# Expert 0's first pair made the fixed first unit of the last phase, with its weights sent from the mixer's last step into memory that both phases share

## The chip, the cores and the metric

The kernel runs on 1 core of one Trainium2 chip. The metric is the device time in microseconds (us). The kernel before took 4290.4 us, the median of three runs (4289.09, 4290.40, 4294.98). A core has five engines: PE (TensorE, matrix products), DVE (VectorE), ACT (ScalarE), POOL (GpSimd) and SP (SyncE, which here only issues transfers). Each engine has its own instruction order; they wait for one another by semaphores. Transfers (DMA) run on 16 DMA engines that all issuing engines share.

## The reference

One transformer-like layer over 8 x 512 tokens of width 512, in float32:

```python
x = x + mamba(layernorm(x))     # in_proj 512->2048, conv of 4 taps, selective scan with
                                # 16 states on 1024 channels, gate, out_proj 1024->512
x = x + moe(layernorm(x))       # 8 experts, top 2 of a softmax router, weights normalised
# moe: h = silu(t @ w1[e]) * (t @ w3[e]);  y = h @ w2[e];  w1, w3: 512x1792, w2: 1792x512
```

The tokens of an expert are sorted together, so that an expert's matrices are used on many tokens at once, and the results are added back into the output with the router's weights.

## The kernel before, in words

There are two phases, each a block of the program with its own on-chip tiles.

**The mixer** (function `mixer`) goes over the tokens in 16 steps of 256 (`STEPS`). Step s scans tile s in 32 pieces (`PIECES`), prepares tile s+1, and finishes tile s-1: output projection, the sum `x1` written to `out` in DRAM (L478), second layer norm, router, and a scatter of each token's normalised row to two places in the DRAM table `rows_d` (L575, POOL). `rows_d` has one region per expert, and in it the rows come in order of arrival. From step 3 on each step also works off one tile of 128 rows of some expert (13 "early" tiles), which leaves fewer for the last phase. A 17th step, s = 16, has no scan and only finishes tile 15. In it the order is a chain: the last output product, the sum x1 on DVE (L1365), its store to `out` (L478, SP), the normalisation in place on ACT (L824, which waits for `x1_stored`, that is for the landing of that store), transposes and router logits on PE (L1024, L1171), choice and ranks on DVE and PE (L1376 to L1446), then four scatters on POOL (L575), and the plan on DVE (L1666 to L1700). The plan counts the rows left for each expert and lists pairs of tiles (2 x 128 rows) and odd tiles (128 rows). Padding rows are written behind each expert's last row by ACT (L956, L960) and SP (L528), one transfer of 257 KB per expert and one for a dummy region.

**The experts** (function `experts`) work off the plan: first all pairs (24 here), then the odd tiles (6 here). A pair is computed with a seven-product scheme (Strassen's, one level): DVE combines the weights (`combine_up`, L2120 to L2125, per quarter q of the width 1792, and `combine_down`, L2136 to L2141), POOL combines the rows (`combine_x`, L1833 to L1838), PE multiplies (`up(j)` for seven column pairs j at L2035, then `down(j)` at L2049), and DVE gathers the products (`chunk(j)`, L2147 to L2157). `up(j)` for j of 2 and more waits for `chunk(j-2)`. Between the phases all engines meet at a barrier, where each first drains. Behind it SP reads four registers from the plan, issues the first quarter of w1 and w3, waits for `scattered` and `padded`, fetches the two tiles of rows (`xr`, L1905), and issues the other quarters and w2:

```python
            n, odd = pairs_filled(sp), odds_filled(sp)
            e0 = sp.value_load(ex_i[0:1, 0:1], min_val=0, max_val=E - 1)
            r0 = sp.value_load(row_i[0:1, 0:1], min_val=0, max_val=DUMMY)
            load_up(0, e0, w13_in)
            sp.wait_ge(scattered, 16 * 2 * TT * STEPS)
            sp.wait_ge(padded, 16 * (E + 1))
            sp.dma_start(xr[:, :, :], both_rows(r0)).then_inc(x_in, 16)
```

DVE starts in this phase with `combine_up(0, q)` for the four quarters, then `chunk(0)`, `combine_down(0, 0)`, `chunk(1)` and so on. SP's order is written out by hand; it issues in that order and waits in that order.

Of the kernel before, what the change touches and what calls it, by code (L numbers as in the profile page):

```python
# [19 lines left out]
F32 = mybir.dt.float32  # L20
# [28 lines left out]
REGION = TOKENS + P  # L49
# [34 lines left out]

def planned(keep):
# [4 lines left out]
def mixer(nc, x, w_in, conv_w, w_x, w_dt, dt_bias, a_log, d_par, w_out, gate, w1, w2, w3, out, rows_d, bc_d, ident, keep,  # L90
          scattered, padded):
    with ExitStack() as ctx:
# [8 lines left out]
        win = [sb(f"win{s}", [P, DC, 2 * P]) for s in range(3)]  # L101
# [14 lines left out]
        uv = sb("uv", [P, 2 * CH * T])  # L116
# [7 lines left out]
        bc = sb("bc", [P, 2 * N, T])  # L124
        dA = [sb(f"dA{s}", [P, PN, T]) for s in range(NB)]
        hs = [sb(f"hs{s}", [P, PN, T]) for s in range(NB)]
# [233 lines left out]
        def _(sp):  # L360
# [56 lines left out]

            def step(s, odd):
# [265 lines left out]
        def _(act):  # L684
# [542 lines left out]
        def _(dve):  # L1227
# [438 lines left out]
            link(dve.tensor_tensor(ends[:, :], ebase[0:1, :], enext, ALU.subtract))  # L1666
            link(dve.tensor_scalar(ci[:, :], ends[:, :], float(P - 1), None, ALU.add))
# [35 lines left out]
def experts(nc, w1, w2, w3, out, rows_d, ident, keep, scattered, padded):  # L1703
    with ExitStack() as ctx:
# [35 lines left out]
        w13_in = [sem(f"w13_in{q}") for q in range(NQ)]  # L1740
        w2_in = [sem(f"w2_in{q}") for q in range(NQ)]
# [130 lines left out]
        def _(sp):  # L1872
# [24 lines left out]

            n, odd = pairs_filled(sp), odds_filled(sp)
            e0 = sp.value_load(ex_i[0:1, 0:1], min_val=0, max_val=E - 1)
            r0 = sp.value_load(row_i[0:1, 0:1], min_val=0, max_val=DUMMY)  # L1900
            load_up(0, e0, w13_in)

            sp.wait_ge(scattered, 16 * 2 * TT * STEPS)
            sp.wait_ge(padded, 16 * (E + 1))
            sp.dma_start(xr[:, :, :], both_rows(r0)).then_inc(x_in, 16)  # L1905
            for q in range(1, NQ):
                load_up(q, e0, w13_in)
            for q in range(NQ):
                load_down(q, e0, w2_in)
# [319 lines left out]
def build(nc, x, w_in, conv_w, w_x, w_dt, dt_bias, a_log, d_par, w_out, gate, w1, w2, w3, out):  # L2229
    rows_d = nc.dram_tensor("rows_d", (DUMMY + 2 * P, RW), F32, kind="Internal").ap()  # L2230
    bc_d = nc.dram_tensor("bc_d", (2 * N, T), F32, kind="Internal").ap()
    with ExitStack() as ctx:
        ident = ctx.enter_context(nc.sbuf_tensor("ident", [P, P], F32))
        keep = [ctx.enter_context(nc.sbuf_tensor(f"keep{i}", [P, CH * N], F32)) for i in range(2)]
        scattered, padded = [ctx.enter_context(nc.semaphore(n)) for n in ("scattered", "padded")]
        mixer(nc, x, w_in, conv_w, w_x, w_dt, dt_bias, a_log, d_par, w_out, gate, w1, w2, w3, out, rows_d, bc_d, ident, keep,
              scattered, padded)
        experts(nc, w1, w2, w3, out, rows_d, ident, keep, scattered, padded)
# [36 lines left out]
```

## Time and profile before

| | |
|---|---|
| runs, us | 4290.4 (4289.09 to 4294.98) |
| the profiled execution, us | 4298.23, its span 4296.5 |
| PE busy | 3894.7 us, 91% of the span |
| DVE, POOL, ACT busy | 3595.8, 2566.5, 2044.4 us |
| mean granted clock of TensorE | 0.958 of full speed |
| mixer | 0 to about 2442 us |
| experts | from about 2442 us to the end |
| PE's largest gap in the trace's second half | 30.7 us, before 2454.15 |

The span runs from the first to the last instruction; the execution's own time is 1.7 us longer. All rows below come from this one execution, which lies 7.8 us above the median of the runs.

### The profile page before, as it was taken

What the parts mean: (1) busy time and instruction counts of PE and PEld (TensorE: products, weight loads), DVE (VectorE), ACT (ScalarE), POOL (GpSimd) and SP (SyncE); (2) the same over time, 40 slices, a digit from 0 to 9 for tenths busy, and PEclk for the clock granted to TensorE, in tenths of its full rate; (3) what the DMA queues carried; (4) which work ended last, traced back from release to release, by engine and by line L of the source; (5) the groups of instructions that cost most, each with busy time, mean ns of one, the idle gap of its engine ahead of it and who ended that gap; (6) DMA issues with size and microseconds to landing.
All of it is one profiled execution on the core that took longest, in us unless ns stands there. A gap on an engine that the chain in (4) does not pass through costs nothing. (4 is left out here: it accounts for less than half of the span.)

```text
span 4296.5 us, 73350 instructions
## 1 busy us (share of the span) xinstructions
PE 3894.7 (91%) x25436; PEld 3379.1 (79%) x25436; DVE 3595.8 (84%) x5245; ACT 2044.4 (48%) x4314; POOL 2566.5 (60%) x2169
## 2 busy tenths in 40 slices
PE   6687889889888988998997599999999999999998
PEld 5565677677767777776776399999999999999886
DVE  5999999999999999999999588878888788788600
ACT  7677777777777777777776111111111111111100
POOL 3677778767877787787776244545545445455300
PEclk9888899999999999999998799999999999999999
DMA  4112353544445454535443455555655655555595
GB/s 162 64 40 94 114 178 114 172 163 134 153 162 170 126 162 159 176 117 173 163 138 113 160 195 183 187 176 181 195 179 183 188 174 187 179 183 191 169 313 194
DMA packets 422582, 694.12 MB, mean 162 GB/s; under 512 B 19680, under 2 KB 209760, under 8 KB 414048
## 3 DMA queue, kind: packets, MB, share of 16 engines
q1 hardware_dynamic: 406160, 655.24, 45.7%
q0 software_dynamic: 14768, 34.41, 4.2%
q8 instruction: 110, 1.80, 0.2%
q10 hardware_dynamic: 1440, 1.81, 0.1%
q14 instruction: 104, 0.85, 0.1%
HBM read 927.54 MB, written 45.95 MB: 227 GB/s over the span
## 5 line engine op out<-in xcount | busy, mean ns | idle before, releaser
L635 POOL TENSOR_TENSOR hs<-hs,bc 128x1024 f32<-128x1024 f32 x512 | 1215.4, 2374 | 312.5 <-DVE hs L1347 290.5
L1347 DVE TENSOR_TENSOR_SCAN hs<-dA,pU 128x1024 f32<-128x1024 f32 x512 | 1168.9, 2283 | 46.2 <-ACT dA L754 24.0
L754 ACT ACTIVATE dA<-delta,aneg 128x255 f32<-128x255 f32 x2048 | 852.2, 517 | 36.4 <-DVE hs L1347 33.5
L1146 PE MATMUL pY<-ident,hs 128*128 128x128 f32 x4096 | 564.2, 285 | 237.6 <-POOL hs L635 237.3
L1146 PEld LDWEIGHTS pY<-ident,hs 128*128 128x128 f32 x4096 | 486.9, 147 | 344.5 <-POOL hs L635 170.5
L1330 DVE TENSOR_TENSOR pU<-pZ,bc 128x1024 f32<-128x1024 f32 x512 | 629.8, 1230 | 30.5 <-issue 0.5
L1822 POOL TENSOR_TENSOR hsum<-hT 128x128 f32<-128x128 f32 x168 | 153.1, 911 | 585.5 <-DVE hT L2174 585.5
L1030 PE MATMUL pM<-xnT,win 128*128 128x256 f32 x1680 | 414.2, 403 | 32.1 <-DMA win<-in_w_in 26.3
L1030 PEld LDWEIGHTS pM<-xnT,win 128*128 128x128 f32 x1680 | 334.8, 205 | 83.2 <-issue 29.5
L2035 PE MATMUL ps<-xT,w1s 128*128 128x128 f32 x2688 | 357.1, 276 | 7.9 <-POOL xt L1838 4.2
L2035 PE MATMUL ps<-xt,su 128*128 128x128 f32 x2688 | 356.8, 276 | 0.0
L2035 PE MATMUL ps<-xt,w3s 128*128 128x128 f32 x2688 | 355.0, 275 | 0.0
L1013 PE MATMUL pE<-xf,ew 128*128 128x128 f32 x2912 | 342.7, 276 | 0.0
L2035 PEld LDWEIGHTS ps<-xT,w1s 128*128 128x128 f32 x2688 | 330.8, 193 | 9.8 <-POOL xt L1838 4.6
L1013 PEld LDWEIGHTS pE<-xf,ew 128*128 128x128 f32 x2912 | 333.8, 193 | 1.7
L2035 PEld LDWEIGHTS ps<-xt,su 128*128 128x128 f32 x2688 | 328.9, 193 | 0.0
L2035 PEld LDWEIGHTS ps<-xt,w3s 128*128 128x128 f32 x2688 | 327.2, 192 | 0.0
L1981 ACT ACTIVATE m<-ps 128x256 f32<-128x256 f32 x168 | 64.0, 381 | 535.3 <-PE ps L2035 535.3
L2049 PE MATMUL ps<-w2s,hT 128*128 128x256 f32 x1008 | 299.9, 379 | 0.0
L1975 ACT ACTIVATE cc<-cc 128x512 f32<-128x512 f32 x168 | 105.9, 630 | 368.5 <-DVE cc L2153 368.5
L2147 DVE TENSOR_TENSOR ut<-ps,m 128x256 f32<-128x256 f32 x168 | 70.6, 420 | 232.9 <-PE ps L2035 231.4
L658 POOL TENSOR_TENSOR xc<-xc,uv 128x512 f32<-128x512 f32 x180 | 216.5, 1203 | 10.9 <-POOL uv L652 5.8
(347 smaller groups left out, 7374.0 us busy)
## 6 DMA issues: line engine op xcount, KB each, us to landing
w1s<-in_w SPq DMA_DIRECT2D x165, 1024.0 KB
w3s<-in_w SPq DMA_DIRECT2D x165, 1024.0 KB
w2s<-in_w SPq DMA_DIRECT2D x165, 1024.0 KB
ew<-in_w SPq DMA_DIRECT2D x273, 512.0 KB, 4.1
win<-in_w_in SPq DMA_DIRECT2D x128, 512.0 KB, 4.7
bc<-bc_d SPq DMA_DIRECT2D x64, 1024.0 KB, 10.3
w1s<-in_w SPq DMA_DIRECT2D x55, 512.0 KB
w3s<-in_w SPq DMA_DIRECT2D x55, 512.0 KB
```

The source lines that it names most:

```text
L635: pool.tensor_tensor(hs[b][:, :, :], hs[b][:, :, :], bc[:, N + g * PN:N + (g + 1) * PN, :], ALU.mult)\
L658: pool.tensor_tensor(xcf[:, 2 * pair:2 * pair + 2, :], xcf[:, 2 * pair:2 * pair + 2, :], y[:, 2 * k:2 * k + 2, k:k + T], ALU.add).then_inc ...
L754: e = act.activation(dA[k % NB][:, i, 1:T], delta[:, c, 1:T], ACT.Exp, scale=aneg[:, c, n:n + 1])
L1013: m = pe.matmul(pEup[:, w, k, :], part[:, d, k * P:(k + 1) * P], exT[:, d, :], start=d == 0, stop=d == DC - 1)
L1030: m = pe.matmul(ps[:, h, :], w[:, d, h * P:(h + 1) * P], rowsT[:, d, :], start=d == 0, stop=d == DC - 1)
L1146: m = pe.matmul(pY[c % 2][:, t * P:(t + 1) * P], hs[k % NB][:, i, t * P:(t + 1) * P], ident[:, :], start=g == 0 and i == 0 and t == 0, sto ...
L1330: dve.tensor_tensor(pU[:, :, :], pDx[:, :].rearrange("p (a t) -> p a t", a=1).to_broadcast([P, PN, T]), bc[:, g * PN:(g + 1) * PN, :], ALU ...
L1347: dve.tensor_tensor_scan(hs[b][:, :, :].rearrange("p n t -> p (n t)"), dA[b][:, :, :].rearrange("p n t -> p (n t)"), pU[:, :, :].rearrange ...
L1822: pool.tensor_tensor(hs[:, j, 0, :], hT[:, j, 2, :], hT[:, j, 3, :], ALU.add).then_inc(hs_step, 1)
L1975: act.activation(cc[j % 2][:, 0:2, :], cc[j % 2][:, 0:2, :], ACT.Silu).then_inc(silu, 1)
L2035: m = pe.matmul(part(s, product)[:, h * P:(h + 1) * P], a(d, cols), b(d), start=d == 0, stop=d == KH - 1)
L2049: m = pe.matmul(part(DOWNS, product), a, b, start=j == 0 and product[1] == 0, stop=j == JN - 1 and (product[1] == 1 or product == M1))
```

## The change

On-chip memory: the mixer's `bc`, `dA`, `hs`, `uv` and `win` and the experts' `w1s`, `w3s`, `w2s` and `xr` become views of one tile `shared`, which lives through both phases. (In a list of instructions of the changed kernel they therefore all read as `shared`.) In the 17th step SP waits until POOL has weighed and PE has summed the last scan piece, and issues all eight transfers of expert 0's w1 and w3 (`first_up`), ahead of the store of x1; after its four padding transfers it issues the four of w2 (`first_down`). In the plan, expert 0's rows left are raised to at least 129, which gives it at least one pair; so the first pair is always expert 0's. For that its region gets 128 more rows of room, and ACT writes one more tile of padding. Behind the barrier SP reads only the row number, waits, and fetches `xr`; it reads the rest of the registers afterwards.

```diff
-REGION = TOKENS + P
+REGION = TOKENS + 2 * P
+WORDS = (W_BC, W_DA, W_HS, W_UV, W_WIN) = (2 * N * T, NB * PN * T, NB * PN * T, 2 * CH * T, 3 * DC * 2 * P)
+def expert_weights(shared):
+    w1s = shared[:, 0:DC * M].rearrange("p (d m) -> p d m", m=M)
+    w3s = shared[:, DC * M:2 * DC * M].rearrange("p (d m) -> p d m", m=M)
+    w2s = shared[:, 2 * DC * M:2 * DC * M + MK * D].rearrange("p (k d) -> p k d", d=D)
...
+            def first_up():
+                sp.wait_ge(weighed, PIECES * STEPS)
+                sp.wait_ge(summed, PIECES * STEPS)
+                sp.wait_ge(e_h, ROUNDS * EARLY)
+                for q in range(NQ):
+                    lo, n = WCH[q]
+                    for ws, w in ((w1s, w1), (w3s, w3)):
+                        sp.dma_start(ws[:, :, lo:lo + n], w[0:D, lo:lo + n].rearrange("(c p) m -> p c m", p=P))\
+                          .then_inc(w13_in[q], 16)
+            def first_down():
+                for q in range(NQ):
+                    lo, n = WCH[q][0] // P, WCH[q][1] // P
+                    sp.dma_start(w2s[:, lo:lo + n, :], w2[lo * P:(lo + n) * P, :].rearrange("(k p) d -> p k d", p=P))\
+                      .then_inc(w2_in[q], 16)
...
+                if s == STEPS:
+                    first_up()
                 if back:
                     hold(x1_ready, TT * r + TT)
                     sp.dma_start(tokens(out, r), rows_of(r)[:, :, 0:D]).then_inc(x1_stored, 16)
...
                 sp.dma_start(rows_d[bass.ds(r, P), :], pad).then_inc(padded, 16)
+            first_down()
             sp.wait_ge(x1_stored, 16 * STEPS)
...
                 act.dma_start(rows_d[bass.ds(r, P), :], pad).then_inc(padded, 16)
+                if e == 0:
+                    act.dma_start(rows_d[bass.ds(r + P, P), :], pad).then_inc(padded, 16)
...
             link(dve.tensor_tensor(ends[:, :], ebase[0:1, :], enext, ALU.subtract))
+            link(dve.tensor_scalar(ends[:, 0:1], ends[:, 0:1], float(P + 1), None, ALU.max))
...
+            r0 = sp.value_load(row_i[0:1, 0:1], min_val=0, max_val=DUMMY)
+            sp.wait_ge(scattered, 16 * 2 * TT * STEPS)
+            sp.wait_ge(padded, 16 * (E + 2))
+            sp.dma_start(xr[:, :, :], both_rows(r0)).then_inc(x_in, 16)
             n, odd = pairs_filled(sp), odds_filled(sp)
-            e0 = sp.value_load(ex_i[0:1, 0:1], min_val=0, max_val=E - 1)
-            r0 = sp.value_load(row_i[0:1, 0:1], min_val=0, max_val=DUMMY)
-            load_up(0, e0, w13_in)
-            sp.wait_ge(scattered, 16 * 2 * TT * STEPS)
-            sp.wait_ge(padded, 16 * (E + 1))
-            sp.dma_start(xr[:, :, :], both_rows(r0)).then_inc(x_in, 16)
-            for q in range(1, NQ):
-                load_up(q, e0, w13_in)
-            for q in range(NQ):
-                load_down(q, e0, w2_in)
```

SP's order in the mixer's last step, before the change (`xc` holds the last tile's x1, the transfer from `in_x` is its residual input):

```order
L434 DMA ew<-in_w 128x2x512
L509 DMA xc<-in_x 128x2x512 [waits x1_ready,y_turned]
L478 DMA out<-xc 128x2x512 [waits x1_ready]
L527 TENSOR_LOAD pad_i [waits pad_idx,pad_set]
```

The same place on SP after the change (`shared<-in_w` are the eight transfers of w1 and w3):

```order
L467 DMA ew<-in_w 128x2x512
L544 DMA xc<-in_x 128x2x512 [waits x1_ready,y_turned]
L441 DMA shared<-in_w 128x4x512 [waits e_h,summed,weighed]
L441 DMA shared<-in_w 128x4x512 x5
L441 DMA shared<-in_w 128x4x256 x2
L513 DMA out<-xc 128x2x512 [waits x1_ready]
L562 TENSOR_LOAD pad_i [waits pad_idx,pad_set]
```

Eight transfers now stand between SP and the store of x1.

SP's order from its last padding transfer over the barrier, before (`rows_d<-xf` is padding, `keep` holds the plan):

```order
L528 DMA rows_d<-xf 128x514
L92 UNCONDITIONAL_BRANCH [waits weights_in,consts_in,x1_stored]
L1871 UNCONDITIONAL_BRANCH [waits barrier_Pool_Activation_PE_DVE_SP_release]
L1793 TENSOR_LOAD keep
...
L1797 TENSOR_LOAD keep
...
L1899 TENSOR_LOAD keep
...
L1900 TENSOR_LOAD keep
...
L1878 DMA w1s<-in_w 128x4x512
L1878 DMA w3s<-in_w 128x4x512
L1905 ISA [waits padded,scattered]
L1905 DMA xr<-rows_d 128x2x514
```

The same place after the change (`shared<-in_w` is w2, `shared<-rows_d` the two tiles of rows):

```order
L563 DMA rows_d<-xf 128x514
L448 DMA shared<-in_w 128x4x512 x3
L448 DMA shared<-in_w 128x2x512
L103 UNCONDITIONAL_BRANCH [waits weights_in,consts_in,x1_stored]
L1905 UNCONDITIONAL_BRANCH [waits barrier_Pool_Activation_PE_DVE_SP_release]
L1932 TENSOR_LOAD keep
L1932 ISA x2
L1935 ISA [waits padded,scattered]
L1935 DMA shared<-rows_d 128x2x514
```

Four transfers of w2 stand ahead of the barrier, and the fetch of the rows comes after one register read and no weights. PE's and POOL's orders are as before; ACT has one more padding transfer, DVE one more instruction in the plan.

## Rows read from the trace of the kernel before

**Rows 1.** Timeline of PE (start us, us, engine, line, tiles, [idle before <- releaser]):

```profile
2394.06 1.91 PE L1146 MATMUL pY<-ident,hs 128*128 128x128 f32 x16
...
2454.15 1.97 PE L2019 MATMUL ps<-ident,xr 128*128 128x128 f32 x8 [30.70 <-DMA xr<-rows_d]
2460.32 2.08 PE L2035 MATMUL ps<-xT,w1s 128*128 128x128 f32 x8 [4.20 <-POOL xt L1838]
...
2473.82 1.06 PE L2035 MATMUL ps<-xt,w3s 128*128 128x128 f32 x8
2475.92 1.13 PE L2035 MATMUL ps<-xT,w1s 128*128 128x128 f32 x8 [1.04 <-DVE cc L2157]
...
2503.85 1.13 PE L2035 MATMUL ps<-xT,w1s 128*128 128x128 f32 x8 [2.69 <-DVE cc L2157]
```

**Rows 2.** The chain that ended last, from 2500 us on (start us, us, what):

```profile
2503.85 8.12 PE ps L2035 x56
...
2534.00 43.77 PE ps L2035 x392
...
2599.80 43.77 PE ps L2035 x392
```

**Rows 3.** The sequencers' instructions of L92, the barrier (engine, count: ns, start):

```profile
L92 POOLq DRAIN  x1: 14330/14330/14330, 2427.8 to 2427.8; - x1
...
L92 DVEq DRAIN  x1: 17/17/17, 2432.1 to 2432.1; - x1
```

**Rows 4.** Timeline of SP's issues:

```profile
2406.82 0.39 SPq L478 DMA_DIRECT2D out<-xc  x1
2425.57 4.59 SPq L528 DMA_DIRECT2D rows_d<-xf  x4
2444.71 0.41 SPq L1878 DMA_DIRECT2D w1s<-in_w  x1
...
2446.21 0.37 SPq L1905 DMA_DIRECT2D xr<-rows_d  x1
...
2448.95 4.48 SPq L1878 DMA_DIRECT2D w3s<-in_w  x1
...
2456.20 2.53 SPq L1878 DMA_DIRECT2D w3s<-in_w  x1
```

**Rows 5.** Timeline of DVE:

```profile
2409.37 0.15 DVE L1266 SCALAR_TENSOR_TENSOR nb<-pZ,mv 128x2 f32<-128x2 f32 x1
...
2431.68 0.17 DVE L1700 CAST keep<-delta 1x39 int32<-1x39 f32 x1
2452.76 1.23 DVE L2120 TENSOR_TENSOR su<-w3s 128x1024 f32<-128x1024 f32 x1 [20.92 <-DMA w3s<-in_w]
...
2466.04 1.23 DVE L2120 TENSOR_TENSOR su<-w3s 128x1024 f32<-128x1024 f32 x1 [1.16 <-DMA w3s<-in_w]
...
2473.24 0.41 DVE L2147 TENSOR_TENSOR ut<-ps,m 128x256 f32<-128x256 f32 x1
...
2478.22 0.42 DVE L2147 TENSOR_TENSOR ut<-ps,m 128x256 f32<-128x256 f32 x1
```

**Rows 6.** Timeline of ACT at the second layer norm of the last tile:

```profile
2409.69 1.52 ACT L824 ACTIVATE xc<-xc,nb,rs 128x512 f32<-128x512 f32 x2 [1.24 <-DMA out<-xc]
```

**Rows 7.** Windows: PE, PEld, DVE, ACT, POOL busy us, PEclk, DMA share, GB/s:

```profile
2397.50:2405.00 7.50, 6.98 (x20) 3.26 (x19) 1.04 (x2) 0.77 (x1) 4.58 (x12) 1.00 0.45 105
...
2425.00:2437.50 12.50, 0.00 (x0) 0.00 (x0) 5.95 (x32) 0.00 (x0) 4.05 (x4) 0.50 0.85 254
2437.50:2442.50 5.00, 0.00 (x0) 0.00 (x0) 0.00 (x0) 0.00 (x0) 0.00 (x0) 0.50 0.00 0
2447.50:2460.00 12.50, 1.97 (x8) 1.57 (x8) 5.17 (x5) 1.08 (x2) 2.59 (x4) 0.50 1.05 392
...
2503.85:2508.80 4.95, 4.95 (x30) 4.95 (x31) 4.85 (x11) 1.01 (x2) 2.99 (x5) 0.66 0.98 372
```

**Rows 8.** Instructions on `xr`, the odd tiles' transposes (ns, first and last start):

```profile
L2074 PE MATMUL ps<-ident,xr x28: 272/273/323, 4047.6 to 4272.2; 128*128 128x128 f32 x28
```

More of the change, by code:

```diff
@@ L82, in ge @@
         eng.wait_ge(sem, value)
+WORDS = (W_BC, W_DA, W_HS, W_UV, W_WIN) = (2 * N * T, NB * PN * T, NB * PN * T, 2 * CH * T, 3 * DC * 2 * P)
[3 more added lines that the diff above has]
+    w2s = shared[:, 2 * DC * M:2 * DC * M + MK * D].rearrange("p (k d) -> p k d", d=D)
+    xr = shared[:, 2 * DC * M + MK * D:2 * DC * M + MK * D + 2 * RW].rearrange("p (r w) -> p r w", w=RW)
+    return w1s, w3s, w2s, xr
 def planned(keep):
@@ L90, in mixer @@
 def mixer(nc, x, w_in, conv_w, w_x, w_dt, dt_bias, a_log, d_par, w_out, gate, w1, w2, w3, out, rows_d, bc_d, ident, keep,
-          scattered, padded):
+          scattered, padded, shared, w13_in, w2_in):
     with ExitStack() as ctx:
@@ L100, in mixer @@
         wgate = sb("wgate", [P, DC, E])
-        win = [sb(f"win{s}", [P, DC, 2 * P]) for s in range(3)]
+        starts = [sum(WORDS[:i]) for i in range(len(WORDS) + 1)]
+        own = [shared[:, starts[i]:starts[i + 1]] for i in range(len(WORDS))]
+        bc = own[0].rearrange("p (n t) -> p n t", t=T)
+        dA = [own[1][:, b * PN * T:(b + 1) * PN * T].rearrange("p (n t) -> p n t", t=T) for b in range(NB)]
+        hs = [own[2][:, b * PN * T:(b + 1) * PN * T].rearrange("p (n t) -> p n t", t=T) for b in range(NB)]
+        uv = own[3]
+        win = [own[4][:, i * DC * 2 * P:(i + 1) * DC * 2 * P].rearrange("p (d q) -> p d q", q=2 * P) for i in range(3)]
         convw = sb("convw", [P, CH, K])
@@ L115, in mixer @@
         state = keep[0][:, :].rearrange("p (c n) -> p c n", n=N)
-        uv = sb("uv", [P, 2 * CH * T])
         vsp, usp = uv[:, 0:CH * T], uv[:, CH * T:2 * CH * T]
@@ L123, in mixer @@
         ysum = [sb(f"ysum{i}", [P, T]) for i in range(2)]
-        bc = sb("bc", [P, 2 * N, T])
-        dA = [sb(f"dA{s}", [P, PN, T]) for s in range(NB)]
-        hs = [sb(f"hs{s}", [P, PN, T]) for s in range(NB)]
         head = keep[1][:, :].rearrange("p (c n) -> p c n", n=N)
@@ L416, in lead_in @@
                     sp.dma_start(dst[tuple([slice(None)] * len(dst.shape))], src).then_inc(weights_in, 16)
+            w1s, w3s, w2s, _ = expert_weights(shared)
+            def first_up():
[12 more added lines that the diff above has]
+                      .then_inc(w2_in[q], 16)
             def step(s, odd):
@@ L1700, in _, with experts @@
             link(dve.tensor_copy(ex_i[:, :], ex[:, :]))
-def experts(nc, w1, w2, w3, out, rows_d, ident, keep, scattered, padded):
+def experts(nc, w1, w2, w3, out, rows_d, ident, keep, scattered, padded, shared, w13_in, w2_in):
     with ExitStack() as ctx:
@@ L1739, in experts @@
         x_in = sem("x_in2")
-        w13_in = [sem(f"w13_in{q}") for q in range(NQ)]
-        w2_in = [sem(f"w2_in{q}") for q in range(NQ)]
         su_step = sem("su_step")
@@ L2234, in build @@
         keep = [ctx.enter_context(nc.sbuf_tensor(f"keep{i}", [P, CH * N], F32)) for i in range(2)]
+        shared = ctx.enter_context(nc.sbuf_tensor("shared", [P, sum(WORDS)], F32))
         scattered, padded = [ctx.enter_context(nc.semaphore(n)) for n in ("scattered", "padded")]
+        w13_in = [ctx.enter_context(nc.semaphore(f"w13_in{q}")) for q in range(NQ)]
+        w2_in = [ctx.enter_context(nc.semaphore(f"w2_in{q}")) for q in range(NQ)]
         mixer(nc, x, w_in, conv_w, w_x, w_dt, dt_bias, a_log, d_par, w_out, gate, w1, w2, w3, out, rows_d, bc_d, ident, keep,
-              scattered, padded)
-        experts(nc, w1, w2, w3, out, rows_d, ident, keep, scattered, padded)
+              scattered, padded, shared, w13_in, w2_in)
+        experts(nc, w1, w2, w3, out, rows_d, ident, keep, scattered, padded, shared, w13_in, w2_in)
 def kernel(**inputs):
```

5 lines of the change are left out of this document (1 added, 4 removed).

## The prediction

> **What bounds the kernel now.** I read the page first: PE is busy 91% of the span, and the 40 slices show one dip, near 2400 us, where the two phases meet. The timeline of PE then gives the place: after its small products of the router PE has nothing until 2454.15, 30.70 us that end with the landing of `xr`, and another 4.20 us until POOL has combined the rows; only at 2460.32 does the first pair begin [rows 1]. The chain that ended last says what a gain there is worth: from 2503.85 on it is PE's products one after the other, 43.77 us for the seven `up(j)` of each pair, 65.80 us from pair to pair [rows 2]. So what moves `up(6)` of the first pair (2503.85) moves the end by as much, and nothing later gives it back or adds to it. The change is to be followed along one path: scan's end, layer norm, router, barrier, `xr`, first pair, `up(6)`.
>
> Three places on it matter. (1) The layer norm of the last tile on ACT starts at 2409.69 [rows 6]; its scale and shift came from DVE at 2409.37 + 0.15 = 2409.52 [rows 5], so the landing of the store issued at 2406.82 [rows 4] was only 0.2 us later than the other input: it costs nothing now, but any delay of it is paid in full. (2) The barrier: DVE drains at 2432.1, but POOL's drain, behind the four scatters, ends at 2427.8 + 14.33 = 2442.1 [rows 3], though the DMA engines carry nothing from 2437.5 to 2442.5 [rows 7]. POOL sets the barrier. (3) The first pair: DVE combines weights as they land (20.92 us idle, then 1.16) and starts `chunk(0)` at 2473.24, later than PE needs it: PE waits 1.04 us for it at 2475.92, and 2.69 us at 2503.85 for a DVE that is still late [rows 1, 5].
>
> **The change part by part: what it delays.** `first_up` can start when PE has summed the last piece, 2394.06 + 1.91 = 2395.97 [rows 1]; say 2396.1. It issues six transfers of 1.049 MB and two of 0.524, 7.34 MB. Are the 0.52 MB of the store held up by them? The nearest rows: the same stream was issued from 2444.71 on; `xr` was issued at 2446.21 behind 2.10 MB of it and landed at 2454.15, 1.39 us after the quarter ahead of it (2452.76), and with 5.24 MB more issued behind it [rows 1, 4, 5]. That is one queue, worked off in order. So the store lands behind all 7.34 MB. Rate: 392 GB/s in 2447.5 to 2460 [rows 7]. Overhead: the first 2.10 MB took 2452.76 - 2444.71 = 8.05 us, of which 2.10/0.392 = 5.35 is data and 2.7 is start and finish. Alone the store would land at 2396.1 + 2.7 + (7.34 + 0.52)/0.392 = 2418.9. But scatters and the last early tile's addition run there too: 0.45 of the engines' time in 7.5 us, 3.4 us, at 105 GB/s, 0.79 MB, which at 392 is 2.0 us [rows 7]. The first gives 2422.3, the second 2420.9. Issuing does not set it: the last of the eight took its turn at 2456.20 + 2.53 = 2458.73, 14.0 us after the first [rows 4], which here is 2410.1, well before the data is through. I take 2420.9: the layer norm and all behind it 2420.9 - 2409.7 = **11.2 us later**, with ends of 9.2 and 12.6. POOL's scatters, the drain and the barrier all hang on that chain and shift with it.
>
> `first_down`: 3.67 MB of w2 behind SP's padding, while POOL's scatters are being written. SP's issue is no cost, since SP is through with padding at 2430.16 and the barrier at 2442.1 waits for POOL. What it may do is slow the scatters, and with them the drain. The DMA engines are 0.85 busy over 12.5 us there already [rows 7]; the scatters share with padding from two queues now, and would share with w2 only for what padding leaves. I take 1 us; ends 0 and 9.4 (all of w2 ahead of the last scatter, 3.67/0.392). ACT's extra padding transfer and DVE's extra instruction (about 0.2 us, as its neighbours) lie under POOL's drain, which ends 10 us after DVE's; if that cover went, they would cost a microsecond.
>
> **What it brings.** All in the times of before, as if the barrier stayed at 2442.1. SP's four register reads and start took until 2444.71, 0.6 us each, so with one read `xr` goes out at about 2443.0 instead of 2446.21. Is the queue free then? The padding and scatters keep the engines busy 0.85 x 12.5 = 10.6 us from about 2426.3 on, one more padding tile adds 0.9 (0.26 MB at 254/0.85, some 300 GB/s), w2 adds 9.4: w2 has landed at 2426.3 + 20.9 + 1.1 = 2448.3 and `xr` 1.4 behind it at 2449.7, instead of 2454.15: **4.5 us earlier**. With an empty queue it would be 2443.0 + 2.7 + 1.35 = 2447.1, 7.0 earlier; the low end is 3.5.
>
> The way from `xr` to `up(0)` (6.17 us: transposes, ACT, POOL) stays, so `up(0)` starts at 2455.8. `up(0)` and `up(1)` took 2473.82 + 1.06 - 2460.32 = 14.56 us, of which `up(1)` 6.25 (43.77/7) and `up(0)`, begun at the lower clock, 8.3. DVE: after its two register reads it begins at 2443.5 with weights that are all there; q2 and q3 took 2473.24 - 2466.04 = 7.2 us, 4.8 and 2.4 by size, so the four quarters take 16.8 and end at 2460.3, 13 us earlier than before. `chunk(0)` then no longer waits for DVE's weights but for `up(0)` (2464.1), and `chunk(1)` for `up(1)` (2470.4), before at 2478.22: **7.8 us earlier**. PE takes `up(2)` at 2470.4 without its 1.04 us, and is ready for `up(6)` at 2495.6; DVE, full from `chunk(1)` on and as long as before (25.6 us), lets it go at 2503.85 - 7.8 = 2496.0. That leaves a wait of 0.4 instead of 2.69. Behind the 2.69 the granted clock was 0.66 over 5 us [rows 7], and 56 products took 8.12 us [rows 2] instead of 6.25; behind the wait of 1.04 nothing of the kind is seen. So I count 1.9 us for a dip that does not come. Gain: 7.8 + 1.9 = **9.7 us**, ends 6.8 (3.5 by `xr`, the rest as above, no clock) and 12.2 (10.3 by a free queue, and the clock).
>
> **Sum.** 11.2 + 1.0 - 9.7 = +2.5 us. The profiled execution would take 4298.2 + 2.5 = 4300.7; it lies 7.8 above the median of the runs, so by the median 4292.9. The change in short: 13 us of weights are taken off DVE's way and 4.5 off PE's, and the same bytes are put in front of the one transfer for which the router waits.
>
> **The rivals.** *The store is not held up* (faster). Its packets would have to pass the weights. Then only the gain is left, 1.0 - 9.7 = -8.7: 4281.7. For it: completion counts per transfer, and the store writes where the loads read. Against: `xr` in the same queue landed in its place, not early. Chance 0.12.
>
> *The scatters are held up by w2* (slower). Place: POOL's drain. Price: up to 9.4 us, so 11.2 + 9.4 - 9.7 = +10.9: 4301.3. It decides as soon as the last scatter lands later than the drain would end anyway; the drain ended 5 us after the engines fell idle, so either there is that much room, or the drain counts from the last landing and has none. For it: the 14.33 us, whose cause no row names. Against: padding stood beside the scatters before as well. The Trainium skill, *DMA: Bandwidth & Descriptors*, section on queues, rings and completion order, speaks for it: each DMA engine takes turns between the queues packet by packet, and a transfer's completion mark "lands only after every earlier write from that SDMA engine, across its queues". By that rule the scatters' marks come behind whatever part of w2 was served before them, and the sum would move from +2.5 towards +10.9. No row here has weights beside scatters, so the trace neither bears it out nor refutes it. Chance 0.13.
>
> *`xr` finds its queue free*: w2 is through by the barrier, for instance because the barrier is later for another reason. The gain is then 12.2, the sum without the 1 us -1.0: 4289.4. Chance 0.10.
>
> *The forced pair is one more unit of work*: if expert 0 had at most 128 rows left, an odd tile (224.6/6 = 37.4 us from 4047.6 to 4272.2 [rows 8]) becomes a pair of 65.8: +28.4 + 2.5, 4321.3. Against: 24 pairs and 6 odd tiles over eight experts are near 6.8 tiles each. Chance 0.02.
>
> **How the numbers follow.** The forecast, 4292.9 with 4288 to 4298 as its own range, has 0.63. About 0.2% (8.6 us) is what a measurement of this kernel can tell from no change, so the bounds are 4281.8 and 4299.0. Faster: most of the first rival and a little of the third, 0.10. Slower: most of the second, the fourth, and the forecast's upper edge with a store that is held longer, 0.14. The rest, 0.76, is no change. The range: from the first rival's upper half to the full price of the second, 4283 to 4302.
>
> **What would show it.** In the profile after: the store's landing (the wait of ACT's layer norm, L860) about 11 us later than the scan's end asks for; right if 23 to 26 us lie between the last L1146-like product and the layer norm (13.7 before), wrong if under 16. POOL's drain ends 32 to 34 us after the layer norm starts (32.4 before); more than 36 is the second rival. From the barrier to the landing of `xr` 7 to 8 us (12 before), with the DMA engines busy up to it; from there 6.2 to `up(0)`. DVE's `combine_up` runs without a wait, 17 us. At `up(6)` a wait under 1 us and a granted clock near 1.0. From there to the end the same length as before, 1792.7 us. The prediction is wrong as a whole if the store lands in 3 us behind the stream, or if any gap in the steady pairs appears.

## The result and the profile after

The changed kernel took 4304.34 us (median of 10 runs, 4301.55 to 4314.38), the kernel before 4294.66 (10 runs, 4289.09 to 4297.10): ratio 1.0026, 95% interval 1.0018 to 1.0034. It is slower, by 9.7 us of the medians, and clear of the noise; 4292.9 had been forecast, with a range to 4302. The ratio and its interval are worked out from all runs, so the ratio is not the quotient of the two medians. A second timing of the same kernel beside its variants gave 1.0035 (1.0021 to 1.0048). One execution of experiment 9 took 17760.9 us and one of experiment 10 took 9054.8 us; neither is in a ratio, and without them the medians of the two are 4291.0 and 4293.9.

Its profiled execution has a span of 4312.6 us, 16.1 more than that of before. Not all of it is the change. The scan's last product ends at 2401.67 instead of 2395.97, in a part whose instructions are the same; over the 13 executions profiled for this study that point came anywhere between 2387.8 and 2401.7. So both traces are compared from the scan's end on, that is from the end of the last product that sums the scan's pieces.

SP's issues in the profile after (start us, us, engine, line, tiles):

```profile
2401.73 15.56 SPq L441 DMA_DIRECT2D shared<-in_w  x8
2417.33 2.58 SPq L513 DMA_DIRECT2D out<-xc  x1
2443.81 4.95 SPq L563 DMA_DIRECT2D rows_d<-xf  x4
2448.80 9.15 SPq L448 DMA_DIRECT2D shared<-in_w  x4
2463.89 0.40 SPq L1935 DMA_DIRECT2D shared<-rows_d  x1
```

These answer to [rows 4]. The store of x1 is issued only when the eight transfers have been: 15.66 us after the scan's end, where it was 10.85 before, so 4.8 us of its delay arise while SP still issues. From its issue to its landing it then takes 10.61 us instead of 2.87, which is the other 7.7. What the DMA engines carried meanwhile, from 2401.7 to 2428 (queue: packets, MB, share of the 16 engines' time; q1 has SP's transfers, q0 POOL's scatters and addition):

```profile
q1 hardware_dynamic: 4496, 7.86, 85.7%
q0 software_dynamic: 304, 0.79, 10.3%
```

Of the 26.3 us the engines spent 22.5 on the weights and the store and 2.7 on POOL's transfers. ACT and DVE beside the stream, with the idle time and its releaser in brackets, answer to [rows 5, 6]:

```profile
2427.94 1.52 ACT L860 ACTIVATE xc<-xc,nb,rs 128x512 f32<-128x512 f32 x2 [13.80 <-DMA out<-xc]
```

```profile
2415.06 0.15 DVE L1304 SCALAR_TENSOR_TENSOR nb<-pZ,mv 128x2 f32<-128x2 f32 x1
...
2464.70 1.22 DVE L2147 TENSOR_TENSOR su<-shared 128x1024 f32<-128x1024 f32 x1 [14.39 <-issue]
...
2474.03 1.75 DVE L2147 TENSOR_TENSOR su<-shared 128x1024 f32<-128x1024 f32 x1
2475.81 1.63 DVE L2149 TENSOR_TENSOR su<-su,shared 128x1024 f32<-128x1024 f32 x1
...
2488.55 0.42 DVE L2174 TENSOR_TENSOR ut<-ps,m 128x256 f32<-128x256 f32 x1 [5.26 <-PE ps L2062]
```

Scale and shift are there at 2415.21, and ACT waits until 2427.94 for the landing alone. Later DVE finds all weights in place and combines without a wait for them; at 2474 its instructions of 1.22 us begin to take 1.6 to 1.75. The drain of POOL at the barrier, answering to [rows 3]:

```profile
L103 POOLq DRAIN  x1: 16857/16857/16857, 2446.0 to 2446.0; - x1
```

And PE, answering to [rows 1]:

```profile
2399.76 1.91 PE L1184 MATMUL pY<-ident,shared 128*128 128x128 f32 x16
...
2470.31 1.97 PE L2046 MATMUL ps<-ident,shared 128*128 128x128 f32 x8 [28.61 <-DMA shared<-rows_d]
2479.74 2.07 PE L2062 MATMUL ps<-xT,shared 128*128 128x128 f32 x8 [7.46 <-POOL xt L1872]
...
2520.50 1.13 PE L2062 MATMUL ps<-xT,shared 128*128 128x128 f32 x8 [0.78 <-DVE cc L2184]
```

The rows land 7.45 us after the drain's end instead of 12.0, as forecast, but from there to the first product it is 9.43 us instead of 6.17: PE waits 7.46 us for POOL's `xt`, before 4.20. The reason stands in POOL's timeline. First the four subtractions of `combine_x` before, then after:

```profile
2457.33 0.77 POOL L1833 TENSOR_TENSOR xt<-xT 128x256 f32<-128x256 f32 x1 [26.28 <-ACT xT L1969]
2458.06 0.72 POOL L1834 TENSOR_TENSOR xt<-xT 128x256 f32<-128x256 f32 x1
2458.74 0.72 POOL L1836 TENSOR_TENSOR xt<-xT,xt 128x256 f32<-128x256 f32 x1
2459.54 0.72 POOL L1838 TENSOR_TENSOR xt<-xT,xt 128x256 f32<-128x256 f32 x1
```

```profile
2473.49 1.21 POOL L1867 TENSOR_TENSOR xt<-xT 128x256 f32<-128x256 f32 x1 [24.31 <-ACT xT L1996]
2474.66 1.70 POOL L1868 TENSOR_TENSOR xt<-xT 128x256 f32<-128x256 f32 x1
2476.32 1.70 POOL L1870 TENSOR_TENSOR xt<-xT,xt 128x256 f32<-128x256 f32 x1
2478.10 1.59 POOL L1872 TENSOR_TENSOR xt<-xT,xt 128x256 f32<-128x256 f32 x1
```

The same work takes 6.20 us instead of 2.93, and that is the whole growth of 3.26 us: from the rows' landing to ACT's copies it is 2.01 us in both traces. In the kernel before, DVE was idle just then, waiting for the second quarter of the weights (from 2457.5 to 2459.55). In the changed kernel it has them and works. A small piece of this stood already in the trace of before: the one DVE instruction that ran beside POOL's last subtraction (2459.54) took 1.79 us, the next one 1.23.

```profile
2459.55 1.79 DVE L2120 TENSOR_TENSOR su<-w3s 128x1024 f32<-128x1024 f32 x1 [2.03 <-DMA w3s<-in_w]
2461.38 1.23 DVE L2122 TENSOR_TENSOR su<-su,w1s 128x1024 f32<-128x1024 f32 x1
```

At `up(6)` PE's wait is 0.78 us instead of 2.69. In the window rows (PE, PEld, DVE, ACT, POOL busy, PEclk, DMA share, GB/s) the granted clock behind it is full, where [rows 7] had 0.66:

```profile
2520.50:2525.50 5.00, 5.00 (x45) 5.00 (x46) 4.90 (x11) 1.01 (x2) 3.06 (x5) 1.00 0.88 301
```

The later pairs are as before, 65.80 us each, in the chain that ended last (answering to [rows 2]):

```profile
2549.02 43.77 PE ps L2062 x392
2614.82 43.77 PE ps L2062 x392
```

The stages, each the difference of two such rows, in us; the last column but one is their sum, from the scan's end to the end of the span. "Forecast" gives the prediction's own stages.

| | scan's end to layer norm | to drain's end | to rows landed | to up(0) | to up(6) | to pair 2 | to the end | sum |
|---|---|---|---|---|---|---|---|---|
| before | 13.72 | 32.44 | 12.02 | 6.17 | 43.53 | 29.99 | 1762.66 | 1900.5 |
| forecast | 24.9 | 33.4 | 7.5 | 6.2 | 40.2 | 28.1 | 1762.7 | 1903.0 |
| after | 26.27 | 34.92 | 7.45 | 9.43 | 40.76 | 28.35 | 1763.75 | 1910.9 |
| difference to before | +12.55 | +2.48 | -4.57 | +3.26 | -2.77 | -1.64 | +1.09 | +10.4 |

The last +1.09 is mostly the first odd tile, whose products in the chain take 28.02 us after and 27.14 before; why is not shown.

### The profile page after: what moved, and what is told of

It is laid out like the page before. It is cut to its first block and busy times, and to the rows that moved or that the text cites. A ratio compares the mean times of both kernels' runs of the same rounds, so it can differ in the third digit from the quotient of the medians.

```text
span 4312.6 us, 73332 instructions
## 1 busy us (share of the span) xinstructions
PE 3900.8 (90%) x25436; PEld 3380.3 (78%) x25436; DVE 3596.9 (83%) x5246; ACT 2044.5 (47%) x4314; POOL 2574.7 (60%) x2169
## 5 line engine op out<-in xcount | busy, mean ns | idle before, releaser
L671 POOL TENSOR_TENSOR shared<-shared 128x1024 f32<-128x1024 f32 x512 | 1215.0, 2373 | 306.5 <-DVE shared L1385 284.5
L1385 DVE TENSOR_TENSOR_SCAN shared<-shared,pU 128x1024 f32<-128x1024 f32 x512 | 1168.5, 2282 | 49.1 <-ACT shared L790 26.8
L790 ACT ACTIVATE shared<-delta,aneg 128x255 f32<-128x255 f32 x2048 | 852.4, 517 | 37.2 <-DVE shared L1385 34.8
L1184 PE MATMUL pY<-ident,shared 128*128 128x128 f32 x4096 | 564.2, 285 | 233.2 <-POOL shared L671 232.9
L1184 PEld LDWEIGHTS pY<-ident,shared 128*128 128x128 f32 x4096 | 486.0, 146 | 341.9 <-POOL shared L671 169.1
L1368 DVE TENSOR_TENSOR pU<-pZ,shared 128x1024 f32<-128x1024 f32 x512 | 629.8, 1230 | 30.5 <-issue 0.5
L1068 PE MATMUL pM<-xnT,shared 128*128 128x256 f32 x1680 | 416.9, 405 | 34.7 <-DMA shared<-in_w_in 28.9
L1068 PEld LDWEIGHTS pM<-xnT,shared 128*128 128x128 f32 x1680 | 336.7, 206 | 86.8 <-issue 32.1
L2062 PE MATMUL ps<-xT,shared 128*128 128x128 f32 x2688 | 356.6, 276 | 8.2 <-POOL xt L1872 7.5
L2062 PE MATMUL ps<-xt,shared 128*128 128x128 f32 x2688 | 355.0, 275 | 0.0
```

The lines of the kernel that those rows point to most:

```text
L671: pool.tensor_tensor(hs[b][:, :, :], hs[b][:, :, :], bc[:, N + g * PN:N + (g + 1) * PN, :], ALU.mult)\
L790: e = act.activation(dA[k % NB][:, i, 1:T], delta[:, c, 1:T], ACT.Exp, scale=aneg[:, c, n:n + 1])
L1068: m = pe.matmul(ps[:, h, :], w[:, d, h * P:(h + 1) * P], rowsT[:, d, :], start=d == 0, stop=d == DC - 1)
L1184: m = pe.matmul(pY[c % 2][:, t * P:(t + 1) * P], hs[k % NB][:, i, t * P:(t + 1) * P], ident[:, :], start=g == 0 and i == 0 and t == 0, sto ...
L1368: dve.tensor_tensor(pU[:, :, :], pDx[:, :].rearrange("p (a t) -> p a t", a=1).to_broadcast([P, PN, T]), bc[:, g * PN:(g + 1) * PN, :], ALU ...
L1385: dve.tensor_tensor_scan(hs[b][:, :, :].rearrange("p n t -> p (n t)"), dA[b][:, :, :].rearrange("p n t -> p (n t)"), pU[:, :, :].rearrange ...
```

## The experiments

All start from the changed kernel. Times are medians; ratios are to the kernel before, run beside them, with their 95% intervals. The sums are those of the table above, from the scan's end on.

**1. The store first.** SP issues the store, then w1 and w3.

```diff
-                if s == STEPS:
-                    first_up()
                 if back:
                     hold(x1_ready, TT * r + TT)
                     sp.dma_start(tokens(out, r), rows_of(r)[:, :, 0:D]).then_inc(x1_stored, 16)
+                if s == STEPS:
+                    first_up()
```

> The changed kernel with one edit: in the mixer's last step SP issues the store of x1 first and expert 0's w1 and w3 behind it. Theory Q (the store waits in SP's queue behind 7.34 MB of weights): the last tile's layer norm starts 13.7 us after the end of the scan's last product instead of 26.3, the rest stays, the time falls by 12.5 us to about 4292 (ratio to before 0.999). Rival: the delay is only moved. The weights, now issued 11 us later, are still in flight when padding and scatters begin, and the drain of POOL grows by what is saved: then the layer norm is early too, but from it to the end of POOL's drain it is 40 us or more instead of 34.9, and the time stays near 4300.

4296.73 us, ratio 1.0006 (0.9997 to 1.0015). The layer norm:

```profile
2407.30 1.52 ACT L860 ACTIVATE xc<-xc,nb,rs 128x512 f32<-128x512 f32 x2 [1.81 <-DMA out<-xc]
```

It starts 14.30 us after the scan's end. 12 us are back in that stage. The drain is 35.62 us after it, not the 40 of the rival; the sum is 1900.2, as before the change, 10.7 us less where 12.5 was expected. The drain, the rows and `up(0)` are each 0.5 to 0.7 us longer than in the table's trace of the changed kernel; its second trace (experiment 5) has the drain at 35.59 too. The weights are still early: they only had to leave the store alone.

**2. The weights stay first, the store goes by another queue.**

```diff
-                if back:
+                if back and s < STEPS:
                     hold(x1_ready, TT * r + TT)
...
+                    if u == 9 and s == STEPS:
+                        act.wait_ge(x1_ready, TT * r + TT)
+                        act.dma_start(out[r * T:(r + 1) * T, :].rearrange("(t p) d -> p t d", p=P),
+                                      rows_of(r)[:, :, 0:D]).then_inc(x1_stored, 16)
```

> The changed kernel with one edit: the last store of x1 is issued by ACT on its own queue, at the same time as before; the weights stay where the change put them, in SP's queue. Theory Q (order in one queue): the store takes turns with the weights and lands 5 to 6 us after its issue; the layer norm starts 16 to 17 us after the scan's end instead of 26.3, the time falls by about 10 us to 4294. Rival B (the DMA engines are full, whatever the queue): the store still waits for most of the 7.34 MB, the layer norm starts 22 us or more after the scan's end, and the time falls by less than 5 us.

4299.57 us, ratio 1.0011 (1.0002 to 1.0020). ACT issues the store and has it 7 us later:

```profile
2404.55 0.46 ACTq L857 DMA_DIRECT2D out<-xc  x1
2411.72 1.52 ACT L864 ACTIVATE xc<-xc,nb,rs 128x512 f32<-128x512 f32 x2 [6.88 <-DMA out<-xc]
```

The layer norm comes 19.36 us after the scan's end: between the two expectations (16 to 17; 22 or more). Another queue gives back 6.9 of the 12.55 us, so the greater part is SP's order, its issuing and its queue together. Of the other 5.6, 1.3 is a later issue: ACT's stands behind its own step of the layer norm, 12.19 us after the scan's end, where SP's was 10.85 before the change, so it was not the same time as expected. The rest, 4.3, is the store's way beside the stream, 7.17 us from issue to landing instead of 2.87. The medians, timed apart, fall by 4.8 us as the rival had it (less than 5), and not by the 10 that the order alone was to give; the sum falls by 6.6, to 1904.3.

**3. w2 behind the rows.**

```diff
-            first_down()
...
             sp.dma_start(xr[:, :, :], both_rows(r0)).then_inc(x_in, 16)
+            for q in range(NQ):
+                lo, m = WCH[q][0] // P, WCH[q][1] // P
+                sp.dma_start(w2s[:, lo:lo + m, :], w2[lo * P:(lo + m) * P, :].rearrange("(k p) d -> p k d", p=P))\
+                  .then_inc(w2_in[q], 16)
```

> The changed kernel with one edit: the four transfers of w2 are issued behind the fetch of the two row tiles, after the barrier, instead of ahead of it. Theory W (w2's transfers both hold POOL's scatters and hold xr): from the layer norm's start to the end of POOL's drain 32.4 us instead of 34.9, from there to the landing of xr 4.0 us instead of 7.5, together 6 us less, unless DVE, whose combine_up has 3.5 us less head start, becomes the later one: at least 3 us less, 4298 to 4301. Rival: the drain has its own length whatever w2 does: it stays at 34.9, and only xr's 3.4 us are won.

4302.37 us, ratio 1.0016 (1.0007 to 1.0025). The drain:

```profile
L103 POOLq DRAIN  x1: 14503/14503/14503, 2439.1 to 2439.1; - x1
```

It ends 32.55 us after the layer norm's start, the old length, and the rows land 4.97 us after it. So w2 ahead of the barrier costs POOL's drain 2.4 us and the rows 2.5. The sum falls from 1910.9 to 1906.3, 4.6 us, where 6 was the most expected; the median is above the 4298 to 4301 expected. The rival, a drain of its own length, is out.

**4. DVE waits for POOL.**

```diff
             for q in range(NQ):
+                if q == 2:
+                    dve.wait_ge(xt_ready, 1)
                 combine_up(0, q)
```

> The changed kernel with one edit: DVE waits for POOL's xt_ready ahead of combine_up(0, 2). Theory P (POOL's four subtractions of the rows took 6.2 us instead of 2.9 because DVE's weight subtractions ran beside them, both reading the same kind of on-chip memory at once): POOL's four take 2.9 us again, xr's landing to up(0) is 6.2 us instead of 9.4, DVE ends its quarters later but still before up(0) ends, and the time falls by 3 us to 4301. Rival: POOL is slow for another reason (the transfers of w2, the tile's place in memory): the four keep their 1.7 us each and the time stays at 4304 or rises by DVE's 2 us.

4304.77 us, ratio 1.0024 (1.0015 to 1.0033). POOL's four:

```profile
2463.10 1.24 POOL L1867 TENSOR_TENSOR xt<-xT 128x256 f32<-128x256 f32 x1 [23.77 <-ACT xT L1996]
2464.30 0.71 POOL L1868 TENSOR_TENSOR xt<-xT 128x256 f32<-128x256 f32 x1
2464.98 0.71 POOL L1870 TENSOR_TENSOR xt<-xT,xt 128x256 f32<-128x256 f32 x1
2465.77 0.72 POOL L1872 TENSOR_TENSOR xt<-xT,xt 128x256 f32<-128x256 f32 x1
```

From 1.70 back to 0.71 us each, but for the first, which still ran beside DVE's last instruction ahead of the wait. `up(0)` is 6.63 us after the rows instead of 9.43, no other stage is longer by more than 0.1 us, and the sum is 1907.4. The transfers of w2 and the tile's place in memory are as they were, so the rival is out. The mechanism is shown in the trace; the median (4301 had been expected) did not show it, so both kernels were timed once more, side by side.

**5 and 6. The changed kernel again, and experiment 4 again.**

> The changed kernel itself, beside its variants on one chip. Expected: 4303 to 4306 us, ratio 1.0015 to 1.003; from the scan's end to the end 1910.9 us within 1.5, whatever the scan's end does, which came between 2388 and 2402 us in the executions seen so far. If the first half is longer in the changed kernel for a reason of its own, its scan end is above 2397 again; if that was chance, it is anywhere between 2388 and 2402.

> The changed kernel with DVE waiting for POOL's rows ahead of combine_up(0, 2), once more, beside the changed kernel in one job: in the job before its trace was 3.5 us shorter from the scan's end on, but its median was not lower. Expected: again 1907.4 us from the scan's end within 1.5 us, and a median 1 to 6 us below the changed kernel's. If the wait costs elsewhere what it saves here, the medians are equal again and some stage of the trace is longer by 3 us.

The changed kernel: 4309.92 us, ratio 1.0035 (1.0021 to 1.0048), sum 1910.3 after a scan's end at 2397.95. With DVE waiting: 4305.95, ratio 1.0028 (1.0017 to 1.0040), `up(0)` 6.47 us after the rows, sum 1907.4. The stage repeats to 0.2 us. The changed kernel's median is above the 4303 to 4306 expected and its ratio above 1.003; its sum is as expected. Its scan's end above 2397, which was to speak for a longer first half, does not settle that: experiment 4, with the same mixer, had 2391.96. Of the medians the first pair (4304.34 and 4304.77, timed apart) shows nothing and the second shows 4.0 us; the intervals of these ratios are 8 to 12 us wide, so 3 us is less than a median here can tell.

**7 to 9. Edits together.** Experiments 1 and 3 (store first, w2 behind the rows); the same with DVE's wait ahead of `combine_up(0, 1)`; the same with the wait ahead of `combine_up(0, 2)`.

> The changed kernel with two edits: the store of x1 ahead of w1 and w3, and w2 behind the fetch of the rows; DVE doesn't wait. If w2 was what lengthened the way from the layer norm to the end of POOL's drain in the kernel with the store first (35.6 us), it is 32.5 to 33.5 again, the landing of the rows comes 4 to 5 us after it, POOL's four subtractions stay slow (6 us), and the time is about 4289. Rival: there the late part of w1 and w3, in flight when padding begins, is what lengthened it; then it stays above 34.5 and the time is 4291 or more.

> The changed kernel with three edits at once: the store of x1 ahead of w1 and w3, w2 behind the fetch of the rows, and DVE waiting for POOL's rows ahead of combine_up(0, 1). If the three costs found (queue 12 us, w2 beside scatters and rows 5 us, DVE beside POOL 3 us) add up, the way from the scan's end to the end is near 1900.2 - 2.5 - 3 - 3 = 1891 us against 1900.5 of the kernel before and 1910.9 of the changed one, and the time is about 4286. Rival: DVE, held until the rows are combined, becomes the later one; then up(0) to up(6) is 42.5 to 44 us instead of 40.8 and the time is 4288 to 4290.

> As the kernel with all three edits, but DVE waits ahead of combine_up(0, 2) instead of (0, 1), so that its second quarter runs beside POOL and only the last two wait. If what counts for POOL is DVE running beside it, POOL's four take between 4 and 6 us here against 2.9 with the earlier wait, up(0) is 1 to 3 us later after the rows' landing, but DVE is 2 us ahead later; the time is within 1.5 us of the other's, 4286 to 4288. If POOL's time doesn't depend on DVE, both are the same.

The columns are the stages of the table above, LN for the layer norm:

| | LN | drain | rows | up(0) | up(6) | pair 2 | end | sum | median | ratio to before |
|---|---|---|---|---|---|---|---|---|---|---|
| 1: store first | 14.30 | 35.62 | 8.00 | 10.01 | 40.29 | 28.36 | 1763.61 | 1900.2 | 4296.7 | 1.0006 |
| 7: and w2 late | 14.25 | 32.85 | 4.85 | 9.72 | 40.37 | 28.36 | 1763.76 | 1894.2 | 4291.7 | 0.9990 |
| 8: and wait at q1 | 14.29 | 32.50 | 4.87 | 6.12 | 42.46 | 29.94 | 1763.88 | 1894.1 | 4289.9 | 0.9987 |
| 9: and wait at q2 | 14.29 | 32.68 | 4.93 | 8.77 | 40.99 | 28.36 | 1763.68 | 1893.7 | 4291.1 | 0.9988 |

The intervals of the last three are 0.9981 to 0.9998, 0.9979 to 0.9996, 0.9979 to 0.9998. Drain and rows fall together once w2 is late (7), so the 35.62 of experiment 1 was w2's, not the late part of w1 and w3. The three versions are equal within the scatter, because DVE's wait pays at one place and charges at another: for experiment 8 the rival came true (42.46 us; 1891 and 4286 had been expected), for 9 POOL's four took 5.54 us, within the 4 to 6 expected. The medians of 7 and 9 are 2.7 us and more above the expected ones. With the early wait POOL is fast, but DVE starts its last three quarters 4.37 us later, and PE waits for it at `up(6)`, with the lower clock behind it:

```profile
2451.92 2.08 PE L2065 MATMUL ps<-xT,shared 128*128 128x128 f32 x8 [4.14 <-POOL xt L1871]
...
2494.38 2.05 PE L2065 MATMUL ps<-xT,shared 128*128 128x128 f32 x8 [2.39 <-DVE cc L2187]
```

```profile
2494.38:2499.40 5.02, 5.02 (x31) 5.02 (x32) 4.92 (x11) 0.94 (x2) 3.06 (x5) 0.67 1.02 389
```

With the later wait one sees the contention end inside POOL's four: DVE's second quarter ends at 2447.04, and only the POOL instruction that starts after it is short.

```profile
2442.87 1.42 POOL L1866 TENSOR_TENSOR xt<-xT 128x256 f32<-128x256 f32 x1 [19.53 <-ACT xT L1999]
2444.26 1.70 POOL L1867 TENSOR_TENSOR xt<-xT 128x256 f32<-128x256 f32 x1
2445.92 1.70 POOL L1869 TENSOR_TENSOR xt<-xT,xt 128x256 f32<-128x256 f32 x1
2447.69 0.72 POOL L1871 TENSOR_TENSOR xt<-xT,xt 128x256 f32<-128x256 f32 x1
```

```profile
2445.30 1.74 DVE L2155 TENSOR_TENSOR su<-shared,su 128x1024 f32<-128x1024 f32 x1
2448.45 1.23 DVE L2150 TENSOR_TENSOR su<-shared 128x1024 f32<-128x1024 f32 x1 [1.41 <-POOL xt L1871]
```

**10. Everything kept but the early weights.** One tile for both phases, the fixed first pair, rows first; w1, w3 and w2 behind the rows after the barrier.

```diff
-                if s == STEPS:
-                    first_up()
...
-            first_down()
...
             sp.dma_start(xr[:, :, :], both_rows(r0)).then_inc(x_in, 16)
+            for q in range(NQ):
+                lo, m = WCH[q]
+                for ws, w in ((w1s, w1), (w3s, w3)):
+                    sp.dma_start(ws[:, :, lo:lo + m], w[0:D, lo:lo + m].rearrange("(c p) m -> p c m", p=P))\
+                      .then_inc(w13_in[q], 16)
...
```

> The changed kernel without its early weights: one shared tile, the fixed first pair and the rows fetched first are kept, but w1, w3 and w2 are issued behind the rows, after the barrier. It shows what is left of the change without the transfers that were moved. Expected if only these matter: the layer norm 13.7 us after the scan's end, the drain 32.4 us after that, rows 4.3 us behind it, but DVE again waits for each quarter as in the kernel before, so that up(6) comes as late as there: 1900 to 1901.5 us from the scan's end, time 4295 to 4297. Rival: the common tile or the larger regions cost something of their own (in the mixer or the later pairs); then it is above 4299, and the part before the scan's end or after the first pair is longer.

4294.08 us, ratio 0.9998 (0.9989 to 1.0007). Stages: 13.72, 31.51, 4.93, 10.85, 44.40, 28.35, 1763.14; sum 1896.9. That is less than expected, 3.6 us below the kernel before: 0.9 in the drain, 1.5 from there to `up(6)`, and 1.6 behind it, where no lower clock follows, less 0.5 up to the end. POOL's four, beside an idle DVE, take 0.72 us each in the common tile. PE now waits for DVE's first quarter at `up(0)`, but no longer for two microseconds or more at any later product:

```profile
2445.76 1.97 PE L2052 MATMUL ps<-ident,shared 128*128 128x128 f32 x8 [22.68 <-DMA shared<-rows_d]
2456.61 2.04 PE L2068 MATMUL ps<-xT,shared 128*128 128x128 f32 x8 [8.88 <-DVE su L2158]
2473.07 1.13 PE L2068 MATMUL ps<-xT,shared 128*128 128x128 f32 x8 [1.88 <-DVE cc L2190]
2501.01 1.13 PE L2068 MATMUL ps<-xT,shared 128*128 128x128 f32 x8 [1.06 <-DVE cc L2190]
```

The windows behind the last two of these waits show the granted clock behind a wait of 1.88 us and behind one of 1.06 us:

```profile
2473.07:2478.00 4.93, 4.93 (x29) 4.93 (x30) 4.86 (x12) 1.01 (x2) 0.00 (x0) 0.65 1.05 384
2501.01:2506.00 4.99, 4.99 (x45) 4.99 (x46) 4.89 (x11) 1.01 (x2) 3.03 (x5) 1.00 0.94 324
```

So the common tile and the forced pair cost nothing that the stages show, and the transfers that were moved account for all of the loss: 1910.9 against 1896.9 with them late. At their best places (7 to 9) they are worth 2.7 to 3.2 us in the traces, which the medians can't tell from nothing.

**11. A fourth edit**, on experiment 8: DVE combines the next pair's first quarter behind `chunk(4)`.

```diff
-                    if j == 3:
+                    if j == 4:
                         combine_up(t + 1, 0)
```

> The kernel with all three edits (DVE waits ahead of combine_up(0, 1)) and a fourth: in every pair DVE combines the next pair's first quarter behind chunk(4) instead of ahead of it. In the kernel with three edits up(6) waited 2.39 us for DVE and a stretch at a lower granted clock followed. If that stall and the clock behind it are what DVE's late start costs, up(0) to up(6) is 40.4 to 41 us instead of 42.46, up(6) to the second pair 28.4 instead of 29.9, and the time falls by 3 us, to about 4287. Rival: the work only moves; DVE is late for the products after up(6) and the down part waits instead: up(6) to the second pair grows by 2 us or more, or the steady pairs leave 65.80 us.

4288.87 us, ratio 0.9989 (0.9980 to 0.9998). `up(0)` to `up(6)` is 39.62 us, to the second pair 28.89 and the pairs stay at 65.80 but for one wait of 0.37 us; sum 1890.5, the shortest. The first is less than the 40.4 to 41 expected, the second more than the 28.4. The stall and the clock behind it are gone, as expected, 3.6 us in the trace; in the medians it is 1.1 against experiment 8, which they can't tell from nothing.

## Why the prediction was wrong, point by point

- **What bounds it: right.** Scan's end, store, layer norm, drain, rows, first pair, then PE alone; no stage after the first pair moved but by 1.1 us. Experiment 1 returns the layer norm's delay and the sum falls by it.
- **The store behind 7.34 MB: right, its size at the top of its bounds.** Forecast 11.2 later (9.2 to 12.6), measured 12.55 and 12.20; the stage of 26.27 us lies just above the 23 to 26 that were to show it. The prediction had two figures for what scatters and the accumulating write take from the stream, 2.0 us by bytes, which it used, and 3.4 by engine time, which would have met the total. That it meets it is luck: by the queues' rows above POOL's 0.79 MB took 2.7 us, SP's 7.86 MB 22.5 us instead of the 20.1 that 392 GB/s gives, and about 1.1 us instead of 2.7 were left for start and finish. Cost of these errors together: 1.4 us. The rival in which the store is not held up (4281.7) is refuted; experiment 2 shows that another queue would have helped, by 6.9 us.
- **`first_down` beside the scatters: right kind, too small.** Taken 1, measured 2.5 in the changed kernel's first trace and 3.2 in its second, and 1.9 to 3.2 over all six traces with w2 ahead of the barrier (rival: up to 9.4); experiment 3 takes 2.4 of it back, and with w2 late the drain is within 0.5 us of before, or shorter. The stage of 34.92 us is above the 32 to 34 forecast and under the 36 of the rival. The Trainium skill's rule (*DMA: Bandwidth & Descriptors*, section on queues, rings and completion order) that completion marks come behind all earlier writes of the same DMA engine pointed the right way. That w2 costs the drain is shown; whether by that rule or by shared bandwidth is not.
- **The rows: right.** 4.5 us earlier forecast, 4.57 measured; a free queue was put at 7.0, and experiment 3 has 7.05 (12.02 less 4.97). The rival in which the changed kernel itself finds its queue free is refuted by this: it would have had some 5 us here and had 7.45.
- **The step that failed: "The way from `xr` to `up(0)` (6.17 us: transposes, ACT, POOL) stays".** It grew by 3.26 us. The 6.17 had been measured while DVE waited for weights, and the change took just that wait away; the prediction let DVE begin at 2443.5 with all its weights, and did not ask who runs beside it then. Experiments 4 and 6 restore 6.6 and 6.5, and experiment 9 shows POOL's time change within one microsecond of DVE's stop. The Trainium skill has the rule (*SBUF — State Buffer*, section on who interferes with whom): a VectorE instruction with two inputs in on-chip memory contends with a GpSimd instruction that reads it, because its second input comes through the read interface that the two engines share; the section calls the shared pair of ports an exclusive lock. The trace agrees nearly: alone, POOL's subtractions follow each other every 0.7 us and DVE's every 1.14; together both go at a pace of about 1.7, a little under the sum of 1.84 that strict turns would give. It was a rule that speaks against this change, and the prediction had not weighed it. DVE's `combine_up` pays too: its four quarters take 18.6 us where 16.8 had been forecast.
- **`up(0)` to `up(6)` and the clock: right.** 40.2 forecast, 40.76 measured; the wait there was 0.78 us, under the 1 us forecast. The dip of the granted clock disappeared with the stall and gave 1.6 us (1.9 forecast), and came back with the stall in experiment 8 (0.67 behind 2.39 us).
- **The sum.** Missed: 3.3 (POOL beside DVE), 1.4 (store), 1.5 (drain), 0.6 (`up(6)`), 0.2 (the clock's gain) and 1.1 (first odd tile), 8.1 us together, which is the distance from +2.5 to +10.4 but for rounding. All erred to the same side. The bounds had been set term by term; the term that failed had none, since it was taken to stay. The time is off by more than the sum, 4304.34 against 4292.9, because the forecast was built on 4290.4, the median of three runs, and ten runs of the same kernel have 4294.66: 4.3 of the 11.4 us are in the base and say nothing of the change. A time no different from before had been given a chance of 0.76, a slower one 0.14.
- **The forced pair: no more work.** 24 pairs and 6 odd tiles as before; PE's products have the same counts on both pages.
- **Open.** A median less the sum and 1.7 us is the time up to the scan's end. It is 2393.2 for the kernel before (its medians lie near 4295.4) and between 2391.7 and 2398.0, on average 2395.2, for the twelve timings of the changed kernel and its variants. So some 2 us may be lost in the first half; against a scatter of the profiled scan's end of 14 us this is not settled. The profiled scan's ends themselves don't show it: on average 2394.7 for the twelve against 2395.97 in the one trace of before.

## What to carry to other kernels

A transfer issued early is paid by whatever comes next in its queue: list the small transfers that an engine waits for, and issue the bulk behind them, not ahead. When a change takes away an engine's wait, look up what ran in that wait on the engine it shares ports with; a duration measured beside an idle neighbour is not the duration beside a busy one. And compare two traces from a common event near the change, since the ends differ by the run's own scatter as much as by a small change.

## What the runs showed of the hardware

- SP's queue is worked in order here: a 0.52 MB store behind 7.34 MB was through 10.6 us after its own issue began (2417.33, layer norm at 2427.94), against 2.9 us with nothing ahead of it [rows 4, 6]; on ACT's queue beside the same stream it took 7.2 us. In the changed kernel the issue itself was also 4.8 us later than the store could have gone.
- Two-input subtractions on DVE (1.22 us) and POOL (0.72 us) slow each other to 1.6 to 1.75 and 1.6 to 1.7 us when they run side by side (the changed kernel and experiment 9).
- POOL's drain behind four scatters of 128 rows took 13.4 to 14.7 us without w2's transfers beside them and 16.4 to 17.6 with them, and ended 5 us after the DMA engines fell idle in the kernel before and 3.5 us after in experiment 7. What it does in that time no trace here names.
- A wait of PE of 1.9, 2.4 or 2.7 us in the first pair was followed by a mean granted clock of 0.65 to 0.67 in the 5 us behind it, in three kernels (experiments 10 and 8, and the kernel before): a part of that stretch ran at the lower of the two levels, 1.2 GHz, where eight products took 1.9 to 2.05 us instead of 1.06. Behind a wait of 0.8 or 1.1 us it was 1.00, all at 2.4 GHz.
